# One transformer kernel: entanglement products of layer 1 moved into the attention's opening, expert bias added in sorted tiles, diagonals and loads reassigned

## The reference

```python
x = _layernorm(x + _L0_attn_ref(x, ...))   # delta-rule values, then causal attention
x = _layernorm(x + _L0_ffn_ref(x, ...))
x = _layernorm(x + _L1_attn_ref(x, ...))
x = _layernorm(x + _L1_ffn_ref(x, ...))    # one expert of 8 for each row
```

```python
e = h @ ent_w[l] + ent_b[l]
ent = e @ ent_pw[l] + ent_pb[l]
```

```python
out = combine[e] * (x @ W[e] + b[e])       # combine: the softmax probability of e
```

## Time and profile before

| what | us |
|---|---|
| median of 3 runs | 976.47 (973.09 to 977.23) |
| the profiled execution | 969.6 |
| its span, first to last instruction | 967.9 |
| TensorE busy in it | 858.6 (89%) |
| VectorE busy | 600.5 (62%) |
| ScalarE busy | 460.8 (48%) |
| GpSimd busy | 288.2 (30%) |

### The profile page before, as it was taken

How to read it: one execution, slowest core, us unless ns; L and a number is a source line. 1 busy time by engine, 2 the same in 40 slices (tenths; PEclk the granted TensorE clock), 3 DMA queues, 4 the chain that set the end, 5 groups by cost and what they waited for, 6 DMA issues and landing times. The chain is left out here.

```text
span 967.9 us, 24865 instructions
## 1 busy us (share of the span) xinstructions
PE 858.6 (89%) x9619; PEld 614.2 (63%) x9619; DVE 600.5 (62%) x2049; ACT 460.8 (48%) x1085; POOL 288.2 (30%) x536
## 2 busy tenths in 40 slices
PE   7896899788889999996989889979999999997883
PEld 4566678677776666755874455554666666686462
DVE  1785489257768888846544535440498899284264
ACT  2563551210004767772335765563267777564064
POOL 0772320156752333330003100000033333511535
PEclk9997997799989999999889998999999999996788
DMA  6043954324420163003001000000000000290561
GB/s 135 1 103 80 252 206 138 104 65 101 110 59 5 38 118 67 2 2 99 1 3 27 1 1 0 1 1 0 1 3 2 2 2 2 72 274 15 206 243 51
DMA packets 56445, 62.73 MB, mean 65 GB/s; under 512 B 9385, under 2 KB 41607, under 8 KB 56072
## 3 DMA queue, kind: packets, MB, share of 16 engines
q1 hardware_dynamic: 47576, 46.93, 18.5%
q0 software_dynamic: 3200, 9.46, 2.7%
q10 hardware_dynamic: 5552, 4.75, 1.6%
HBM read 31.84 MB, written 25.99 MB: 60 GB/s over the span
## 5 line engine op out<-in xcount | busy, mean ns | idle before, releaser
L995 DVE CUSTOM_DVE_ANT_0 l_masked_scores<-psum,mask_q_rows 128x384 bf16<-128x384 f32 (+3 forms) x512 | 220.1, 488 | 29.2 <-PE psum L934 25.5
L1011 ACT ACTIVATE kT_or_probs<-psum 128x512 f32<-128x512 f32 (+1 forms) x192 | 87.4, 531 | 115.8 <-PE psum L920 114.7
L1024 POOL TENSOR_SCALAR_AFFINE_SELECT l_probs<-l_probs 128x256 f32<-128x256 f32 x128 | 50.5, 406 | 223.0 <-ACT l_probs L1011 222.8
L1011 ACT ACTIVATE l_probs<-psum 128x512 f32<-128x512 f32 (+1 forms) x192 | 87.3, 531 | 29.7 <-PE psum L920 28.6
L934 PE MATMUL psum<-kb_heads,q_heads 32*128 32x384 f32 (+3 forms) x512 | 92.5, 459 | 0.0
L934 PE MATMUL psum<-l_k_heads,l_q_heads 32*128 32x512 f32 (+3 forms) x512 | 90.5, 452 | 0.7 <-PEq L46 0.7
L920 PE MATMUL psum<-b_slot_rows_or_q_and_max,kb_heads 32*128 32x512 f32 (+3 forms) x512 | 87.3, 457 | 0.7 <-DVE b_slot_rows_or_q_and_max L1001 0.7
L920 PE MATMUL psum<-l_q_and_max,l_k_heads 32*128 32x512 f32 (+3 forms) x512 | 86.2, 450 | 0.7 <-DVE l_q_and_max L1001 0.7
L1024 POOL TENSOR_SCALAR_AFFINE_SELECT kT_or_probs<-kT_or_probs 128x256 f32<-128x256 f32 x128 | 50.5, 406 | 95.1 <-ACT kT_or_probs L1011 95.0
L767 POOL TENSOR_TENSOR v_new_and_ones<-v_and_k_rows_or_heads 32x128 f32<-32x128 f32 x128 | 55.1, 448 | 28.9 <-DVE v_and_k_rows_or_heads L745 25.3
L920 PEld LDWEIGHTS psum<-b_slot_rows_or_q_and_max,kb_heads 32*128 32x128 f32 x512 | 53.4, 186 | 12.6 <-ACT kT_or_probs L1011 5.1
(11 more groups left out here) (376 smaller groups left out, 1854.7 us busy)
## 6 DMA issues: line engine op xcount, KB each, us to landing
sorted_scratch<-l1p_zeros SPq DMA_DIRECT2D x23, 257.0 KB, 6.1
x_rows<-in_L_attn_x_dram SPq DMA_DIRECT2D x32, 128.0 KB, 8.5
gram_scratch<-rows_32k SPq DMA_DIRECT2D x4, 1024.0 KB, 6.1
rows_32k<-v_new_and_ones SPq DMA_DIRECT2D x64, 64.0 KB, 2.6
heads_scratch<-rows_32k SPq DMA_DIRECT2D x2, 1024.0 KB, 5.4
heads_scratch<-q_kb_T SPq DMA_DIRECT2D x2, 1024.0 KB, 5.3
x_rows<-in_L_ffn_ent_w_dram POOLq DMA_DIRECT2D x2, 1024.0 KB, 8.2
block_A<-gram_scratch SPq DMA_DIRECT2D x16, 128.0 KB, 2.7
```

What stands on the lines that cost most here:

```text
L995: last = self.nc.vector.tensor_tensor_reduce(out=self.junk[:, n % 4, o:o + w], in0=self.g.ps[:, self.row_bank(G, u, i), o:o + w], in1=self ...
L1011: self.nc.scalar.activation(self.PT[:, G % 2, 2 * (u % 2) + i, o:o + w], self.g.ps[:, self.e_bank(G, u, i), 0:w], ACT.Exp, scale=SCALE).th ...
L1024: last = self.nc.gpsimd.affine_select(out=d, in_=d, pattern=[[0, 2], [1, P]], compare_op=ALU.is_ge, fill=0.0, base=0, channel_multiplier=-1)
```

## The change

Four edits:

1. **Diagonals.** For the last four of the 16 gram units (from `SHARED` = 12 on) ScalarE copies all four squares, and VectorE none; it goes on to its scaling and inverse.
2. **Ent path of layer 1.** Its transposes stay in the inverse stage and go to a place of their own (`g.ewT1`, over layer 0's ent_pw), its bias comes next, behind the wait for the ent_pw load; its two sums of products leave the stage. They stand in the attention's opening: in unit 0 the idle products stay, in units 1 to 7 come 2 or 3 of the 16 products in place of the idle ones, and in unit 8 TensorE waits until ScalarE has copied both results, then issues the idle set.
3. **Ent loads.** GpSimd issues the three 1 MB loads at its end in the projections, once x has been transposed, and not at the start of the inverse stage.
4. **Expert bias.** No transposes of `combine`, no bias products for chunks, no additions; a scattered row has 258 numbers (x, 1/sum, row number). The bias of all experts lies on one partition, and every tile has one more product, of one contraction row of ones with the expert's bias, ahead of the wait for the tile's transposes. The fill products wait until GpSimd has issued 12 of the 16 scatters.

The diff, cut to its core:

```diff
+            pool.wait_ge(xT_ps, NT)
+            load_ent(pool, g, g.ew, "ent_w", 0, g.ent_ld)
+            load_ent(pool, g, g.epw, "ent_pw", 0, g.ent_ld)
+            load_ent(pool, g, g.ew, "ent_w", 1, g.ent_ld)
...
+        SHARED = 2 * NP - NP // 2
+        def blocks_copied(i, units):
+            return 2 * min(units, SHARED) if i == 0 else 2 * units + 2 * max(0, units - SHARED)
...
-                        pe.wait_ge(at_ok[i], 2 * (u - 1))
+                        pe.wait_ge(at_ok[i], blocks_copied(i, u - 1))
...
             ent_wT(1)
-            ent_products(1)
+            pe.wait_ge(epw_ld, 16)
+            ent_bias(1)
...
-            for u in range(2 * NP):
+            for u in range(SHARED):
                 dve.wait_ge(gram_ps, u + 1)
...
-                for b in range(2, B):
+                for b in range(2 if u < SHARED else 0, B):
...
+            def beside_first_rows(n):
+                if n == 0:
+                    idle_row_products(nc, g, 0, 0, 2)
+                elif n < LEAD - 1:
+                    for i in range(2 * KF * (n - 1) // (LEAD - 2), 2 * KF * n // (LEAD - 2)):
+                        ent_product(i // KF, i % KF)
+                else:
+                    pe.wait_ge(g.e_ok, len(E_STEPS))
+                    idle_row_products(nc, g, 0, 0, 2)
...
+            for m in range(KD):
+                act.wait_ge(g.e_ps, E_AT[f"W1_{m}"] + 1)
+                nc.scalar.copy(g.Wf2[:, 1, m, :], ent_psum(f"W1_{m}")[:, 0:D]).then_inc(g.e_ok, 1)
             att.scalar(act)
...
         for n in range(LEAD):
             step([], row_unit(n))
-            idle_row_products(self.nc, self.g, 0, 0, 2)
+            beside_first_rows(n)
...
-XW = 2 * D + 2
+XW = D + 2
...
-            for c in range(NT):
-                if c % G4 == 0:
-                    pe.wait_ge(ct_sb, c // G4 + 1)
-                if c >= 2:
-                    pe.wait_ge(xb_ok, c - 1)
-                nc.tensor.matmul(ps[:, 6 + c % 2, 0:D], cT[:, c, :], be[:, :], start=True, stop=True).then_inc(b_ps, 1)
-            pe.wait_ge(xb_ok, NT)
+            pe.wait_ge(most_sent, 1)
...
+                nc.tensor.matmul(ps[:, 4 + t % 2, 0:D], ones[0:1, :], be[:, bass.ds(e, 1), :].rearrange("p e n -> p (e n)"), start=True, stop=False)
                 pe.wait_ge(t_sb, t + 1)
...
             for c in range(NT):
-                pool.wait_ge(xb_ok, c + 1)
+                if c == NT - 4:
+                    nc.gpsimd.memset(order[:, 0:1], 0.0).then_inc(most_sent, 1)
```

More of the change, by code:

```diff
@@ L396, in phase_delta @@
         eye, own = sb("slot_eye_and_minus_one", [P, HD + 1]), sb("own_columns", [P, 2, B * HD])
+        g.e_ps, g.e_ok, g.epw_ld = (both.enter_context(nc.semaphore(n)) for n in ("ent_step_psum", "ent_step_read", "ent_pw_loaded"))
         delta_blocks(nc, g, ps, UW, VC, IS, eye, own)
@@ L516, in ent_products, with ent_bias @@
                     for k in range(KF):
-                        nc.tensor.matmul(o[:, 0:D], ewT[:, k, m * P:(m + 1) * P], g.epw[l][:, k, :], start=(k == 0), stop=False)
+                        nc.tensor.matmul(o[:, 0:D], ewT[l][:, k, m * P:(m + 1) * P], g.epw[l][:, k, :], start=(k == 0), stop=False)
                     nc.tensor.matmul(o[:, m * P:(m + 1) * P], g.idf[:, :], g.idf[:, :], start=False, stop=True).then_inc(e_ps, 1)
+                ent_bias(l)
+            def ent_bias(l):
                 o = bank(f"b{l}")
@@ L694, in delta_scan, with ent_psum, ent_product @@
         WB = B * HD
+        def ent_psum(step):
+            return ps[:, 2 + E_AT[step] - E_AT["W1_0"], :]
         @block.tensor
         def _(pe):
+            def ent_product(m, k):
+                o = ent_psum(f"W1_{m}")
+                nc.tensor.matmul(o[:, 0:D], g.ewT1[:, k, m * P:(m + 1) * P], g.epw[1][:, k, :], start=(k == 0), stop=False)
+                if k == KF - 1:
+                    nc.tensor.matmul(o[:, m * P:(m + 1) * P], g.idf[:, :], g.idf[:, :], start=False, stop=True).then_inc(g.e_ps, 1)
+            def beside_first_rows(n):
[7 more added lines that the diff above has]
+                    idle_row_products(nc, g, 0, 0, 2)
             for s in range(NB2):
@@ L2266, in _ @@
             nc.scalar.activation(pr[:, :, :], lg[:, :, :], ACT.Exp).then_inc(ex_ok, 1)
-            for q in range(NG):
-                act.wait_ge(ct_ps, q + 1)
-                nc.scalar.copy(cT[:, q * G4:(q + 1) * G4, :], ps[0:E, 2 + q, :].rearrange("p (c m) -> p c m", c=G4)).then_inc(ct_sb, 1)
             act.wait_ge(sorted_st, 16 * NT)
```

58 lines of the change are left out of this document (22 added, 36 removed).

## The result

The changed kernel takes 975.33 us (median of 20 runs) where the kernel before, run beside it, takes 968.65 us (20 runs). The ratio is 1.0053, 95% interval 1.0030 to 1.0076: about 5 us slower by that ratio (6.7 between the two medians), where 4 us faster was forecast.

The account below looks back on a forecast made before the run. TensorE was busiest; the inverse stage's last store was held by the ent path, the expert layer by GpSimd's scatter, then TensorE's tiles. -4.7 + 3.3 - 2.8 = -4.2 us on 976.47 gave 972.3, range 966 to 980.

Parts of the forecast that it names:

- Part 5: Expert layer: tiles begin 3.4 us earlier, step 1.58 us with TensorE the loop's only bound; -2.8 us.
- tile loop overloaded: Rival, expert tiles: extra product brings its own register step and weight load, none overlapping; step 1.95, total +3.5, chance 0.13.
- Part 3: First attention's opening: layer-1 ent products replace idle ones, partly hidden in TensorE's waits for VectorE; +3.3 us, bounds 1.5 to 4.5.
- Part 1: Inverse stage, diagonals: ScalarE's extra copies start the ent path 2.6 us later; VectorE's inverse gains 0.8 us.
- Part 2: Inverse stage without layer-1 ent products: chunk products at 164.6, second inverse's store at 173.2; -4.7 us, bounds -6 to -2.
- stage not relieved: Rival, inverse stage: lower TensorE clock through the ent path or late fourth gram store; -2 instead of -4.7, chance 0.15.
- Part 4: Projections: three ent loads issued there by GpSimd; nothing gained, up to +1 us if they slowed the heads' stores.

Follow-up runs that it names:

- m_k128: Kernel before with only the expert layer's edit, its bias product made from 128 contraction rows instead of one; 968.69 us, ratio 0.9992 to the kernel before.
- m_nobias: Kernel before with only the expert layer's edit, its bias product left out (experts' bias missing from the output); 967.85 us, ratio 0.9987 to the kernel before.
- d_only: Kernel before with only the diagonals' edit (last four gram units' diagonals copied by ScalarE alone); 978.99 us, ratio 1.0078 to the kernel before.
- q_only: Kernel before with only the three 1 MB ent loads issued at the end of the projections; 966.05 us, ratio 1.0038 to the kernel before.
- the last group: Changed kernel and three variants timed on one chip beside the kernel before (965.09 us); the changed kernel took 974.49 us, ratio 1.0099.

## Why the prediction was wrong

**Part 5 failed, by one term.** The scatter began 1.2 us after the cast of the slots, the tiles 3.3 us earlier, both nearly as forecast. The step was forecast at 1.58 us from 0.435 for the bias product. It is 1.90, and over 22 steps that is 7.0 us: the last scatter came 50.6 us after the first transposes, not 44. The text said that no row showed one contraction row, and took the price of the columns. It could have had the price: the kernel before has such a product in its feed-forward part, a bias product of four contraction rows and 256 columns among full ones:

```profile
625.23 1.13 PE L1800 MATMUL psum<-stage_matrix,v_and_k_rows_or_heads 128*128 128x256 f32 x4
626.29 0.69 PE L1801 MATMUL psum<-stage_bias_rows,ffn_deviationsT 4*128 4x256 f32 x2
626.92 1.13 PE L1800 MATMUL psum<-stage_matrix,v_and_k_rows_or_heads 128*128 128x256 f32 x4
```

Start to start, the pair takes 626.92 - 626.29 = 0.63 us and the four around it 1.06, where the chain showed 0.87 for four. That is 1.69 us where the columns give 1.30, 0.39 more, and `m_k128` measured 0.38. With it the forecast's own step is 1.09 + 0.435 + 0.39 = 1.9. The rival *tile loop overloaded* had this size (1.92, 1.95) and the right side, but another cause: `m_k128` has the same register step and as many weight loads, and its bias product costs 0.44.

The Trainium skill, TensorE: Matmul & The Clock Gate, section Why this matters for your kernels, says that a single product of 32 contraction rows takes as long as one of 128. By that rule the forecast left its 0.435 as it was. No run times such a product by itself. For a stream that changes between the two it does not hold: between full products the one-row product costs 0.38 us more than the full one, and the measurement decides. The same page of the Trainium skill, section Part 3: Packing small matmuls, says that weight loads overlap with products in flight only where the row groups differ. The trace agrees at the changes, where the load of a one-row product starts with the product. It does not agree between full products, which hold the same rows and whose loads still start 0.11 to 0.22 us ahead in `m_k128`, beside the product in flight. Why nothing is loaded ahead at a change, no run here shows.

**The base of Part 5 was partly an accident.** The forecast took 1.51 us as the mean step before, 6.3 us over 22 steps more than 1.224 each, and explained it by loads of long rows that kept ScalarE's output buffer. That stop is real and went with the halved rows, but it is 1.90 of the 6.3 us. Other stops, which `m_nobias` and `m_k128` have with half the bytes, come and go between executions, and TensorE runs at the lower clock behind them (2.07 us where four instructions take 1.13). The loop before takes 41.1 to 46.9 us from one execution to the next.

**Part 3's mechanism was right, its size not** (+5.8 for +3.3, outside its bound of 4.5). The sixteen products and two identities take 8.6 us, not 7.6: four instructions stand 1.06 us, again 0.2 above their columns, between row scores of 32 contraction rows. The row scores pay the same: a set of 512 columns between full products takes 1.06 us in place of 0.87 (289.05 to 290.11), one of 256 columns 0.63 in place of 0.44. Over the seven sets behind full products (6.05 us by their starts, 4.80 by their columns) and the transposes of the maxima that is 1.4 us, which the forecast had at nothing. With both, 3.3 + 1.0 + 1.4 = 5.7 of the 5.8 us are there: the idle products and the wait that went were worth what the forecast said, and only the changes between 32 and 128 contraction rows were missing.

**Part 1** forecast 2.6 us for the ent path and got 4.0 to 4.5. Its own rows give 3.1 for the copies, not 2.5, since the last unit before took ScalarE 1.18 and not 1.74; the rest is the clock, which fell behind TensorE's wait. It forecast 0.8 us gained for VectorE's start; the start came 1.2 to 1.7 earlier in the changed kernel, but not at all with the diagonals alone (`d_only`) or the early loads alone (`q_only`). That it takes both together is likely, and not run by itself.

**Part 2** forecast the chunk products 57.2 us after the first gram product (164.6); they came after 58.5 and 61.5, by Part 1's lateness and by the bias at 1.2 GHz, 7.6 us where 4.0, at most 5.5, stood in the text. It forecast the store at 173.2, that is 65.8 us after the first gram product. It goes at 66.9 in one profile and at 70.0 in the other, where it still stands behind SyncE's loads, as the rival *stage not relieved* had it. The stage gained 0.1 to 5.7 us, 2.2 between the means (88.1, 91.1 and 91.5 against 92.4); without the diagonals' edit (89.2 and 89.7) the move is worth about 3. **Part 4** held: nothing.

The sum with what was measured: stage -2.2, opening +5.8, begin of the tiles -3.3, tiles +3.7 to +9.5, by what the loop before took. That is +4 to +10, and the times say +5, and +9.5 in the last group.

## What to carry to other kernels

A product with few contraction rows between full ones is not cheap: price it by a row of the same kind, and look for one in the whole trace, not just in the stage that changes; if the memory is there, give it all 128 rows. Work that leaves an engine's busy stretch should go where that engine waits for a transfer, not where it is the feeder of another. An edit that makes TensorE wait can cost more than its wait, when what follows runs at the lower clock, as in `d_only`.

## What was not expected of the hardware

- A product of one or four contraction rows (256 columns, 32-bit) between products of 128 adds 0.38 us: 0.62 for the pair itself in place of 0.44, 0.1 each on the products around it. At a change the weight load starts with its product, and not ahead of it. Row scores of 32 contraction rows next to full products show the same: 1.06 for four instructions in place of 0.87, on either side.
- The tile loop stops for about 3 us once or twice in some executions: TensorE's product is issued, its count reaches VectorE and ScalarE some 2.6 us later (927.0, an end that is modelled, and 929.6 in `m_nobias`). The output buffers are excluded as a cause, since ScalarE's copy there waits for none, and the loads' length isn't needed for it; what it is stays open.
